# Audio tower: VectorE's odd projection swap placed ahead of the reciprocal of the next pair's row sums

## What is computed

```python
q = apply_rope(split_heads(x @ Wq))
k = apply_rope(split_heads(x @ Wk))
v = split_heads(x @ Wv)
sim = jnp.einsum('bid,bjd->bij', q, k) * d ** (-0.5)
sim = jnp.where(causal[None], sim, -jnp.inf)
attn = jax.nn.softmax(sim, axis=-1)
out = jnp.einsum('bij,bjd->bid', attn, v)
out = merge_heads(out) @ Wo + bo
```

## Time and profile before

| | |
|---|---|
| runs before, us | 1754.49, 1753.79, 1750.00; median 1753.79 |
| profiled execution, us | 1756.17, its span 1754.3 |
| mean granted TensorE clock | 0.924 of full speed |
| busy of the span | PE 84%, PEld 78%, DVE 70%, ACT 56%, POOL 53% |
| attention | about 104 to 830 us of the span |

### The profile page before, as it was taken

The page is one execution under the profiler, slowest core; times in us unless marked ns, Lnnn a source line. Parts: engine busy times, 40 slices in busy tenths (PEclk is TensorE's granted clock), DMA queues, the critical chain, the costliest instruction groups (busy, mean ns, idle before and its releaser), DMA issues. The chain is left out here.

```text
span 1754.3 us, 30236 instructions
## 1 busy us (share of the span) xinstructions
PE 1476.7 (84%) x10725; PEld 1374.2 (78%) x10725; DVE 1223.8 (70%) x2590; ACT 989.0 (56%) x2138; POOL 927.4 (53%) x750
## 2 busy tenths in 40 slices
PE   5389999999999999995699999999988746789039
PEld 4279888888888888885699999999987745788039
DVE  7548677777777777774256666666588489459896
ACT  4547675757575757572455555555543444459552
POOL 4468475858585858572567677776755623000000
PEclk8679999999999999997799999999999968899569
DMA  7490000000000100001665555555544321003313
GB/s 241 147 309 19 19 19 28 28 28 28 28 28 25 31 25 14 25 13 34 193 167 142 138 146 136 148 135 149 140 122 107 66 89 43 11 0 133 110 51 113
DMA packets 86126, 150.38 MB, mean 86 GB/s; under 512 B 7992, under 2 KB 63608, under 8 KB 85720
## 3 DMA queue, kind: packets, MB, share of 16 engines
q1 hardware_dynamic: 75464, 134.62, 24.7%
q0 software_dynamic: 10512, 13.83, 4.6%
HBM read 111.88 MB, written 49.91 MB: 92 GB/s over the span
## 5 line engine op out<-in xcount | busy, mean ns | idle before, releaser
L1589 POOL TENSOR_TENSOR expert_w_low<-expert_raw,expert_w_high 128x768 fp32r<-128x768 f32 x152 | 288.5, 1948 | 172.1 <-ACT expert_w_high L1414 167.0
L855 ACT ACTIVATE expert_raw<-psum,neg_max 120x376 f32<-120x376 f32 (+2 forms) x384 | 176.9, 486 | 106.0 <-DVE neg_max L1041 103.8
L1561 DVE TENSOR_TENSOR expert_act_low<-expert_act,expert_act_high 128x384 fp32r<-128x384 f32 x152 | 140.0, 921 | 79.6 <-ACT expert_act_high L1452 79.0
L1452 ACT ACTIVATE expert_act_high<-expert_act 128x384 fp32r<-128x384 f32 x152 | 79.8, 525 | 204.1 <-DVE expert_act L1556 202.7
L967 POOL TENSOR_TENSOR qk_low<-rotated,qk_high 128x376 fp32r<-128x376 f32 x128 | 127.0, 992 | 95.2 <-ACT qk_high L848 95.2
L1373 PE MATMUL psum<-slots_high,expert_w_high 128*128 128x384 f32 x608 | 161.0, 346 | 16.7 <-DVE expert_act L1556 15.4
L1064 DVE TENSOR_TENSOR pt_low<-psum,pt_high 128x752 fp32r<-128x752 f32 x128 | 120.4, 941 | 69.9 <-ACT pt_high L864 69.5
L1373 PE MATMUL psum<-slots_low,expert_w_high 128*128 128x384 f32 x608 | 157.0, 339 | 0.0
L1373 PE MATMUL psum<-slots_high,expert_w_low 128*128 128x384 f32 x608 | 156.7, 338 | 0.0
L1384 PE MATMUL psum<-expert_w_high,expert_act_high 128*128 128x256 f32 x456 | 134.5, 295 | 11.6 <-ACT slot_out L1434 9.9
L997 POOL TENSOR_TENSOR rotated<-rotated,expert_raw 128x376 f32<-128x376 f32 x128 | 127.7, 998 | 14.5 <-POOL expert_raw L993 0.5
(11 more groups left out here) (305 smaller groups left out, 4380.6 us busy)
## 6 DMA issues: line engine op xcount, KB each, us to landing
expert_raw<-in_experts SPq DMA_DIRECT2D x152, 384.0 KB, 3.1
x_slots<-in_c_slots SPq DMA_DIRECT2D x4, 3168.0 KB, 27.8
slot_rows<-x_slots SPq DMA_DIRECT2D x19, 396.0 KB, 4.5
up_spill<-held SPq DMA_DIRECT2D x5, 1128.0 KB, 5.0
held<-up_spill SPq DMA_DIRECT2D x5, 1128.0 KB, 5.7
attn_x<-tok_xt SPq DMA_DIRECT2D x6, 752.0 KB, 4.0
x_parts<-attn_x SPq DMA_DIRECT2D x6, 752.0 KB, 4.6
patch<-in_patches SPq DMA_DIRECT2D x8, 376.0 KB, 6.8
```

Of the source, the lines that this page charges most:

```text
L855: last = act.activation(probs[0:ni, h % 2, at:at + P * it + ni], score_bank(h % 2, it), ACT.Exp, bias=neg_max[0:ni, h % 2, it:it + 1], acc ...
L1561: dve.tensor_tensor(act_hl[1][:, g % 2, :], act_f[:, g % 2, :], act_hl[0][:, g % 2, :].bitcast(F32), ALU.subtract).then_inc(low_made, 1)
L1589: pool.tensor_tensor(w[1][:, g % RING, :], raw[:, g % RAW, :], w[0][:, g % RING, :].bitcast(F32), ALU.subtract).then_inc(w_low, 1)
```

## The change

In DVE's `step` the odd `swap_pairs` is called in front of `inverses` instead of behind it. No instruction is added or removed and no semaphore or buffer changes. The call is made in the 56 steps of batches 0 to 6 and in pairs 0 to 4 of batch 7, 61 steps in all; in the other three the order of the remaining calls is as before.

```diff
                     keep_inverse(b, c)
                     if b == LAST and c == ROUTE_PREFIX:
                         place_rows(b - 1)
+                    if projects:
+                        swap_pairs(b, ahead + 1)
                     if more or c + 1 < PAIRS:
                         inverses(b, c + 1)
-                    if projects:
-                        swap_pairs(b, ahead + 1)
                     scale_out(b, c)
```

## The result

Over six runs each, the changed kernel took 1744.9 us (1743.12 to 1746.24) and the kernel before 1755.03 us (1750.0 to 1756.48). The ratio is 0.9946 with a 95% interval of 0.9932 to 0.9959: 10.1 us less, 7.2 to 11.9 by the interval. The forecast was 1746.2 with a range of 1743.0 to 1753.5. It took 7.6 off a median of three runs, 1753.79; with six runs the kernel before has 1755.03. The profiled execution of the changed kernel has a span of 1744.3, against 1754.3.

A forecast was written before the change was run, and what follows sets the result against it. The prediction took a closed ring of ScalarE and VectorE, not TensorE, to set most steps. It summed 6.24 + 0.55 + 0.8 = 7.6 us off the 1753.79 median, giving 1746.2, range 1743 to 1753.5.

The forecast's parts named there:

- (1): VectorE's swap starts in its idle 0.89 behind the copy; TensorE's wait is released 1.0 us earlier, its gap gone.
- (2): VectorE's reciprocal, now behind the swap, starts 0.07 us late, covered by 0.38 of slack before ScalarE's spread.
- (3): Pairs 0 to 3, batches 1 to 7: TensorE's gap only moves to its wait for the low part; no gain.
- (4): Pairs 4 and 5, batches 1 to 6: TensorE comes 0.23 plus 0.52 earlier, so 0.75 us passes into the ring.
- (5): Ends of batches 1 to 6: 0.29 us more, making 1.04 in each of six batches, 6.24 us.
- (6): Batch 0, without router: 0.35 us in seven steps plus 0.2 at its end, 0.55 us.
- (7): Batch 7, pair 4: VectorE's copy follows the reciprocal sooner, 0.89 us less, of which 0.8 is taken.
- The clock rival: Batch 7: without TensorE's idle 0.70 the clock stays at 2.4 GHz; 1.7 us less, 1744.5; chance 0.20.
- Contention: The swap reads PSUM beside ScalarE's exponentials; cost taken as zero; as the slower rival, 1761, chance 0.07.
- TensorE the bound after all: Rival: every one of about 61 gaps of 0.5 us comes back, 30 us, giving 1723; chance 0.03.
- the lead lost: Rival: TensorE's lead of 0.75 meets another wait in pair 5; only batches 0 and 7 gain, 1753; chance 0.17.
- the ring: ScalarE and VectorE handing work to each other in a closed loop, said to set most steps' length, 8.79 us in batch 4.

The follow-up runs named there:

- the experiment that used it up: Changed kernel with VectorE's reciprocal moved one place further back, behind the copy L1052 and the output bank's scaling multiply: 1776.43 us in one run.
- the repeat: The kernel before, with no edit, profiled a second time: 1753.12 us, span 1751.3.
- An experiment that takes a known amount out of the other ring: Changed kernel with ScalarE's row scaling and its copy of the router's turned tile moved ahead of tile 2's exponentials: 1731.46 us, ratio to before 0.9875.

## Why the prediction was right, point by point

The time was right: 7.6 forecast, 7.2 in the steps, 8.5 to 10.1 in the medians. That 1746.2 lies only 1.3 from 1744.9 is in part luck: the saving was forecast 2.5 below the first pair of medians, and the base, the median of the first three runs, lay 1.2 low as well. The 1.5 to 3 us that no step accounts for are in no term of the prediction either. Most terms of the sum can be read off.

(1) *The swap moves into the idle time.* Right, and the bank is empty 1.15 earlier rather than 1.0. The gap is gone (turn to projection 0.60).

(2) *The reciprocal.* Right. It isn't late at all, and the slack it was given, 0.38, is 0.43 by the experiment that used it up. In the changed kernel the spread waits for it 0.5 us in all, in two steps.

(3) *Pairs 0 to 3 gain nothing.* Right: no step of pairs 0 to 3 of batches 1 to 7 moved by more than 0.03, and the change in pairs 0 to 2 alone left those steps where they were. The runs add what the rows of before couldn't show: the cover is at least 0.3 to 0.5 wide in pairs 0 to 2, and in pairs 3 and 4 it is used up as soon as ScalarE's copy stands where it waits for TensorE.

(4) *Pairs 4 and 5.* The mechanism was right and the size somewhat off: 0.75 was said, 0.63 came (0.06 + 0.57). ScalarE's wait fell by 0.60. The term that was mis-sized is the 0.23 at the mix of pair 4. TensorE did come early enough to wait there, 0.17 by the row, but from a mix that it had waited for it is 420.48 - 419.23 = 1.25 to the turn, not the 422.89 - 421.75 = 1.14 of before: 0.11 was lost again right behind the wait. The first matmul behind the wait is the longer one, 0.44 against 0.33. The gap itself gave 1.09 - 0.60 = 0.49 and not 0.52.

(5) *The ends of the batches.* 0.29 forecast, 0.30 measured. Per batch 1.04 became 0.95, so 6.24 became 5.7.

(6) *Batch 0.* 0.55 forecast, 0.58 measured, but two errors cancel: seven steps gave 0.26, not 0.35, and the end 0.32, not 0.2. The high part follows the spread by 169.06 - 168.64 = 0.42.

```profile
168.64 0.55 ACT L869 ACTIVATE inv_wide<-inv_sum 128x384 f32<-128x384 f32 x1
169.06 0.83 ACT L864 ACTIVATE pt_high<-psum 128x752 fp32r<-128x752 f32 x1
```

(7) *Batch 7.* VectorE's copy follows the reciprocal by 0.29 instead of 1.10, 0.8 less as taken; TensorE's idle 0.70 is gone, and the step is 0.9 to 1.0 shorter when it is compared with the other executions of the old order.

```profile
769.93 0.19 DVE L1048 RECIPROCAL inv_sum<-row_sum 128x6 f32<-128x6 f32 x1
770.22 0.28 DVE L1058 COPY inv_rows<-psum 128x120 f32<-128x120 f32 x1
```

*The clock rival.* Its time (1744.5) is the one nearest to the measured 1744.9, and the profile pair looks like it: no idle 0.70, no fall behind it, and 2.56 us less in the step, 1.67 of them beyond the usual. That its time came nearest is luck all the same. The runs bear out half of it. The fall does go with the idle time (four of six with it, none of seven without). What was mis-sized is the price. It was read off one execution, and in five others the same idle time costs 0.1 or nothing in the step. Even the 1.67 was worth only 0.8 at the end of the attention, where the clock's later fall was shorter than in the repeat (some 3.4 us at 1.2 GHz against 6.8). The Trainium skill (TensorE: Matmul & The Clock Gate, HAM oscillation) ties such falls to idle gaps of TensorE, in its example waits for transfers that are longer than the 0.70 here; the rows agree as to the gap, and show beside it that the same gap in the same kernel brings a fall in one execution and none in the next.

*Contention.* None to be seen, so zero was the right value. The exponentials' durations (least, median, greatest, in ns) over the attention, before and then changed:

```profile
L855 ACT ACTIVATE expert_raw<-psum,neg_max x376: 360/495/605, 110.1 to 784.5; 120x376 f32<-120x376 f32 x63, 128x256 f32<-128x256 f32 x63, 128x128 f32<-128x128 f32 x62
```
```profile
L855 ACT ACTIVATE expert_raw<-psum,neg_max x381: 357/493/599, 110.4 to 784.6; 120x376 f32<-120x376 f32 x64, 128x256 f32<-128x256 f32 x64, 128x128 f32<-128x128 f32 x63
```

These are all exponentials of the attention. The last one of each step (128x256), the one beside which the swap now lies, takes 0.50 in the median in both kernels. By the rule that the prediction cited (the Trainium skill, SBUF — State Buffer, Who interferes with whom) ScalarE waits for no other engine at SBUF's ports, and the runs agree: 495 against 493 ns.

*TensorE the bound after all,* and *the lead lost.* Neither: pairs 0 to 3 kept their length, and the lead reached pair 5.

## What to carry to other kernels

An engine that is 96% busy and waits 24 us for one line need not gain anything when that wait goes: follow it from the gap to the engine's next wait, and if that one is for the ring, the gap is covered there. Count only the places where another engine waits for it (here ScalarE's one wait of 1.21 in a batch, and the batch's end). An experiment that takes a known amount out of the other ring shows which ring binds and how wide the cover is, and here it led to 14 us more than the change itself gave (1745.49 to 1731.46). It also shows what binds next: GpSimd in pair 1, TensorE in pairs 3 and 4.

Don't take the price of a clock fall from one execution: look at a second profile of the same kernel before a term of the sum rests on it.

## What the runs showed that was not expected

- The same kernel, profiled twice, differs by 1.67 us in one step (11.39 and 9.72). Behind the same idle 0.70 of TensorE (0.69 or 0.70 in six executions) the clock was at 1.2 GHz for some 6.8 us in one execution (worked out from the granted clock of the windows above), for some 3.4 us in three others, and not at all in two.
- What lies behind the attention has two lengths some 2.7 us apart (919.1 to 919.9, and 922.0 to 922.6), in either order, and the granted clock 20 to 40 us behind L1186 tells them apart (1.00, and 0.94 or 0.95). The attention's first high part starts at 117.7 to 120.3. A comparison of two spans can be off by several microseconds for these reasons alone, where single steps of the same kernel repeat within 0.04 outside batch 7's pair 5. The sixty steps up to pair 4 of batch 7 together repeat within 0.5.
- A mix that TensorE had to wait for takes 0.11 longer to the next turn than one that it ran into without waiting. For the odd heads, in both profiles of before and both of the changed kernel, it is 1.24 to 1.26 wherever a wait is shown, and 1.14 to 1.16 wherever the first matmul is the short one (some 0.34).
